# A sorted-row store for the last stage's gathers: 832 rows gathered once and loaded per tile, in place of 960 gathers

## The chip, the core and the metric

The kernel runs on one core of a Trainium2 chip. The metric is the device time of one execution in microseconds (us), from start to end. Engines are named as in the profile: PE is TensorE (PEld its weight loads), DVE is VectorE, ACT is ScalarE, POOL is GpSimd and SP is SyncE, which here issues DMAs and computes nothing. A "q" behind an engine's name marks its sequencer, which waits, branches, does arithmetic on registers and issues DMAs.

## What is computed

Four graph layers follow each other on 6250 nodes of 128 features and 106250 edges (`src`, `dst`, sorted by `dst`): a gated graph network, a hypergraph layer, an attention layer and an edge network. The change lies in the last one:

```python
def _L3_gnn_ref(x, edge_index, We1, be1, We2, be2, Wn1, bn1, Wn2, bn2):
    src, dst = (edge_index[0], edge_index[1])
    e_in = jnp.concatenate([x[src], x[dst]], axis=-1)
    edge_new = _mlp(e_in, We1, be1, We2, be2)
    agg = jax.ops.segment_sum(edge_new, dst, num_segments=x.shape[0])
    mesh_new = _mlp(jnp.concatenate([x, agg], axis=-1), Wn1, bn1, Wn2, bn2)
    return x + mesh_new
```

The first product of the edge network splits in a source part and a target part. The kernel makes both per node, so an edge needs one row of each: their sum, through a ReLU, is added up over the edges of a target.

## The kernel before

**Sorted rows and tiles.** Early in the kernel the edges are sorted by a key of their source's place (near, middle, far) and their target's block of 128 nodes, and stored in DRAM (`edges_halves`) as 832 rows of 128 edges. A tile is one row seen from one block of targets: a row that spans two blocks is in two tiles. There are T = 960 tiles, taken in 120 chunks of CH = 8. For each tile, `pair_idx` names its row and `pair_blk` its block; in the second hyperedge pass POOL fetches each tile's 128 edges (line 1770), VectorE splits them in target and source (`pair_steps`, lines 983 to 999), and TensorE turns them so that `local` (target inside the block) and `gather_idx` (source) stand with edges on partitions (`pairs_kept`).

**Source rows.** The attention pass (pass 5) writes the source part of 13 groups of nodes to a DRAM `table` (SP, line 546). POOL gathers by `gather_idx` (line 1148), one indirect DMA for the 128 edges of a tile, 64 KB. `early_pool` runs beside the attention pass: 20 pairs of chunks, 16 gathers each, into `x_fm`, where each pair waits for the groups that its sources need (`early_need`, line 1162) and is stored to `early_rows` in DRAM by POOL (line 1158). `edge_pool` then gathers the other 80 chunks straight into a ring of HOT = 4 slots, each slot when line 1306 has used it.

**The stage between.** After the attention pass ScalarE copies turned node rows to `x_fm` (line 1984, 25 chunks); copy 10 waits until all early stores have landed, as it overwrites their place. Then all engines meet, and the edge stage starts.

**The edge stage.** Six chunks make a turn in the order "DDEDDE" (D: direct, E: from `early_rows`); 20 turns. Per chunk, SP loads the targets inside the block, broadcast to all partitions (line 1198, 512 KB of f32), and in E chunks the stored rows (line 1191). ScalarE makes from the targets a one-hot matrix (`turned_hots`, lines 1219 and 1221); TensorE multiplies it with the block's target part (line 1272); VectorE adds the gathered source rows (line 1306, twice per chunk, counted in `edge_pre`); ScalarE applies the ReLU (line 1236); TensorE sums by target (lines 1248 and 1252) and VectorE adds to `acc` (line 1314). TensorE and VectorE read block numbers from a table in SBUF to registers (`registers`, line 477). SP's waits for one chunk come in program order, ahead of its DMAs. Behind the stage follow the node network, the last normalization and the output.

Of the kernel before, what the change touches and what calls it, by code (L numbers as in the profile page):

```python
# [20 lines left out]
P = 128  # L21
# [18 lines left out]
HOT = 4  # L40
# [28 lines left out]
EARLY = 40  # L69
EARLY_PAIRS = EARLY // 2  # L70
DIRECT = CHUNKS - EARLY
TURN = "DDEDDE"
LOOPS = EARLY // TURN.count("E")
PER_TURN = TURN.count("D")
SPARE = DIRECT - PER_TURN * LOOPS
assert EARLY % 2 == 0 and LOOPS * TURN.count("E") == EARLY and SPARE >= 0 and HOT == PER_TURN
# [80 lines left out]
def gnn(nc, d):  # L157
    ctx = ExitStack()
    with ctx:
# [49 lines left out]
        block_row = block_of[0:1, :]  # L209
# [82 lines left out]
        early_need = sb("early_need", [1, EARLY_PAIRS], I32)  # L292
        early_f = sb("early_f", [1, EARLY_PAIRS])

# [45 lines left out]
        pair_rows, pair_key = pair_rows.bitcast(I32), pair_src.bitcast(I32)  # L340
# [4 lines left out]
        early_ring = [x_fm[:, TW + KT * P + k * CH * P:TW + KT * P + (k + 1) * CH * P] for k in range(4)]  # L345
        early_twos = [x_fm[:, TW + KT * P + 2 * k * CH * P:TW + KT * P + 2 * (k + 1) * CH * P] for k in range(2)]
# [10 lines left out]
        early_rows = dram("early_rows", (EARLY, P, CH * P))  # L357
# [4 lines left out]
        local_rows = dram("local_rows", (TP, P))  # L362
# [22 lines left out]
        def S(name):  # L385
            if name not in made:
# [5 lines left out]
        half_landed = [S(f"half_landed{k}") for k in range(2 * HOT)]  # L392
        early_in = [half_landed[2 * (HOT - 2 + k)] for k in range(2)]
        direct_landed = [Count(half_landed[k], (16 * 2 * CH * ((EARLY_PAIRS + 1 - (k // 2 - HOT + 2)) // 2)
                                                if k in (2 * HOT - 4, 2 * HOT - 2) else 0)) for k in range(2 * HOT)]
# [5 lines left out]
        early_stored = Count(S("pairs_in"), 16 * TG)  # L401
# [41 lines left out]
        def col(j):  # L443
# [5 lines left out]
        targets = [stage[:, (4 + k) * CH * P:(5 + k) * CH * P] for k in range(2)]  # L449
        assert 6 * CH * P <= NBP * W and HOT * CH * P <= NP and HOT * CH <= 2 * SC  # L450
        row_ring = [big[:, NP + k * CH * P:NP + (k + 1) * CH * P].rearrange("p (t f) -> p t f", f=P) for k in range(HOT)]
        EARLY_SLOTS = TURN.count("E")
        early_ready = [big[:, NP + (HOT + k) * CH * P:NP + (HOT + k + 1) * CH * P].rearrange("p (t f) -> p t f", f=P)
                       for k in range(EARLY_SLOTS)]
# [9 lines left out]
        assert (HOT + EARLY_SLOTS) * CH * P + T // WINDOW <= NP and GW <= EC and GROUPS < LOOPS and 2 * len(TURN) % 3 == 0  # L464
        assert len(TURN) % HOTS == 0 and len(TURN) % 2 == 0
# [38 lines left out]
        early_landed = [Count(tile_landed[k], 16 * -(-(turns_before(len(MODES)) - k) // RING)) for k in range(EARLY_SLOTS)]  # L504
# [35 lines left out]
        def matrix_sp(p, sp):  # L540
# [31 lines left out]
            if p == SCALED:  # L572
                scale_load((GROUPS - 1) % 2, GROUPS - 2)
                sp.wait_ge(S("pair_values"), 1)
                sp.dma_start(local_rows.rearrange("(g p) e -> p g e", p=P), pair_f).then_inc(S("local_stored"), 16)
                sp.wait_ge(S("local_stored"), 16)
# [261 lines left out]
        def matrix_pe(p, pe):  # L838
            mode = MODES[p]

            def body(n, g, first_turn, i):
                wait(pe, S("group_out"), groups_before(p) + n - 1 + LOOPED * i)
                for t in range(TURNS):
# [4 lines left out]
                    if p == SCALED and n == 0 and t == 10:  # L848
                        pe.wait_ge(S("pair_values"), 1)
                        for v, values in enumerate((pair_f, pair_src)):  # L850
                            for b in range(TG):
                                last = nc.tensor.transpose(ps[:, 1 + 2 * v + b // 4, (b % 4) * P:(b % 4 + 1) * P],
                                                           values[:, b, :], ident[:, :])
                        last.then_inc(S("pair_flipped"), 1)
# [64 lines left out]
        def matrix_dve(p, dve):  # L919
# [61 lines left out]
            def pair_keys():  # L981
                one = chain(dve)
                dve.wait_ge(S("pairs_in"), 16 * TG)
                one(nc.vector.tensor_scalar(pair_key, pair_rows, (1 << KEY_BITS) - 1, None, ALU.bitwise_and))
                one(nc.vector.tensor_scalar(pair_rows, pair_rows, KEY_BITS, None, ALU.logical_shift_right))

            def pair_locals():
                for b in range(TG):
                    last = nc.vector.tensor_scalar(pair_f[:, b, :], pair_key[:, b, :], pair_blk[:, b:b + 1], None, ALU.subtract)
                chain(dve)(last)  # L990

            def pair_from():
                chain(dve)(nc.vector.tensor_scalar(pair_src, pair_f, 0.0, None, ALU.is_ge))

            def pair_below():
                chain(dve)(nc.vector.scalar_tensor_tensor(pair_src, pair_f, float(P), pair_src, ALU.is_lt, ALU.mult))

            def pair_sources():
                nc.vector.tensor_tensor(pair_src, pair_rows, pair_src, ALU.mult).then_inc(S("pair_values"), 1)
            pair_steps = [pair_keys, pair_locals, pair_from, pair_below, pair_sources]  # L1000

            def pairs_kept():
                dve.wait_ge(S("pair_flipped"), 1)
                for v, out in enumerate((local, gather_idx)):
                    for j in range(2):
                        last = nc.vector.tensor_copy(out[:, j * 4 * P:(j + 1) * 4 * P], ps[:, 1 + 2 * v + j, :])
                last.then_inc(S("pair_flipped"), 1)
# [67 lines left out]
        class Spot:  # L1075


            def __init__(self, i, h, x=0, nodes_done=False):
                self.i, self.h, self.x = i, h, x
                self.nodes = not x and not nodes_done and h == len(TURN) - 1  # L1080
                self.nodes_done = nodes_done or x
                self.u = len(TURN) * i + h + x
                self.known = isinstance(i, int)
                self.direct = x > 0 or TURN[h] == "D"
                if x:
                    self.k = PER_TURN * LOOPS + x - 1
                    self.u = len(TURN) * LOOPS + x - 1
                    self.use = self.k // HOT
                else:
                    before = TURN[0:h].count(TURN[h])  # L1090
                    self.k = TURN.count(TURN[h]) * i + before
                    self.use = i
                self.slot = (TURN[0:h].count("D") if self.direct else TURN[0:h].count("E")) if not x else self.k % HOT
                self.par = (x - 1) % 2 if x else h % 2
                self.hot = (x - 1) % HOTS if x else h % HOTS
                self.at = x - 1 if x else h
                self.pair = (len(TURN) * LOOPS + x - 1) // 2 if x else len(TURN) // 2 * i + h // 2
                self.chunk = EARLY + self.k if self.direct else self.k
                self.first = self.known and not x and i == 0 and h == 0
                self.last = x == SPARE if SPARE else self.known and i == LOOPS - 1 and h == len(TURN) - 1  # L1100

            def after(self):
                if self.x:
                    return Spot(0, 0, self.x + 1)
                if self.h + 1 < len(TURN):
                    return Spot(self.i, self.h + 1)
                return Spot(0, 0, 1) if self.known and self.i == LOOPS - 1 else Spot(self.i + 1, 0)

            def before(self):
                if self.x > 1:  # L1110
                    return Spot(0, 0, self.x - 1)
                if self.x == 1:
                    return Spot(LOOPS - 1, len(TURN) - 1)
                return Spot(self.i, self.h - 1) if self.h else Spot(self.i - 1, len(TURN) - 1)

            def q_bank(self, g):
                return ps[:, 4 + (2 * self.at + g) % 3, :]

            def rows(self):
                return row_ring[self.slot] if self.direct else early_ready[self.slot]  # L1120

            def wait_rows(self, eng, g):
                if self.direct:
                    wait(eng, direct_landed[2 * self.slot + g], 64 * (self.use + 1))
                elif g == 0:
                    wait(eng, early_landed[self.slot], 16 * (self.use + 1))

        def edge_turns(eng, body):

            def turn(i, nodes_done=False):  # L1130
                for h in range(len(TURN)):
                    body(Spot(i, h, 0, nodes_done))
# [7 lines left out]
        def direct_at(k):  # L1140

            if k >= PER_TURN * LOOPS:
                return len(TURN) * LOOPS + k - PER_TURN * LOOPS
            spots = [h for h in range(len(TURN)) if TURN[h] == "D"]
            return len(TURN) * (k // PER_TURN) + spots[k % PER_TURN]

        def gather(pool, out, t):
            return nc.gpsimd.indirect_dma_start(out, None, table[0:N, :], bass.IndirectOffsetOnAxis(gather_idx[:, t:t + 1], 0))  # L1148

# [1848 lines left out]
```

## Time and profile before

| what | value |
| --- | --- |
| time, median of 3 runs | 4566.51 us (4559.16 to 4568.67) |
| the profiled execution's own time | 4566.38 us |
| its span, first to last instruction | 4564.6 us |
| busy, PE / DVE / ACT / POOL | 84% / 72% / 51% / 58% |
| POOL in the last 850 us (from 3700) | 0.95 us busy of each 1.26 |
| chain that ended last, largest part | POOL line 1148, 13% into `big` and 5% into `x_fm` |

The page gives each engine's busy time as a share of the span; stages differ much in what limits them. The chain is followed back from the last instruction to what released each step. In a group's line the idle time stands behind the bar, with what ended most of it. All stretches below are in us from the span's start.

### The profile page before, as it was taken

The numbers are of one execution on the slowest core, as the hardware profiler recorded it, in microseconds if no ns is written. First come the engines' busy times: TensorE is split into PE (matmuls) and PEld (weight loads), VectorE is DVE, ScalarE is ACT, GpSimd is POOL, SyncE is SP. The second block draws the span as 40 slices with busy tenths as digits, with TensorE's granted clock in tenths as the row PEclk, the third lists the DMA queues.
The fourth block names the chain that finished last, engine by engine and source line by source line (L and its number), as shares of the span: only waits on it lengthen the run. The fifth ranks groups of instructions, "written<-read, shape, count | busy, mean of one in ns | idle before, by whom it ended". The sixth has DMA issues, their size and how long they took to land. (4 is left out here: it accounts for less than half of the span.)

```text
span 4564.6 us, 82617 instructions
## 1 busy us (share of the span) xinstructions
PE 3855.8 (84%) x24477; PEld 3205.3 (70%) x24478; DVE 3281.3 (72%) x7175; ACT 2334.1 (51%) x3120; POOL 2669.8 (58%) x2702
## 2 busy tenths in 40 slices
PE   5888408998889998998699799789999988888777
PEld 3666207776667776777488588479999976666665
DVE  6887898897788888887776543557887865555556
ACT  0000306665455555553555555578888855555545
POOL 3777777777377777777730000000477777777773
PEclk8999759999999999999799799789999989888888
DMA  9920009998538845982598788214677755454543
GB/s 381 373 95 1 3 0 329 366 368 298 200 116 282 269 144 179 291 280 88 173 299 297 171 296 297 99 56 143 194 235 242 242 164 163 151 160 158 158 154 97
DMA packets 362569, 914.64 MB, mean 200 GB/s; under 512 B 113834, under 2 KB 138524, under 8 KB 362291
## 3 DMA queue, kind: packets, MB, share of 16 engines
q1 hardware_dynamic: 213570, 645.89, 42.8%
q10 hardware_dynamic: 58609, 180.13, 10.3%
q0 software_dynamic: 90112, 85.23, 7.9%
q8 instruction: 136, 2.23, 0.2%
q14 instruction: 142, 1.16, 0.1%
HBM read 701.50 MB, written 209.51 MB: 200 GB/s over the span
## 5 line engine op out<-in xcount | busy, mean ns | idle before, releaser
L1765 POOL DMA_INDIRECT edges_halves<-local,gather_idx x832 | 850.9, 1023 | 304.7 <-issue 253.4
L1704 POOL DMA_INDIRECT adj_t<-cell_val,cell_at x832 | 815.6, 980 | 321.6 <-issue 321.6
L878 PE MATMUL ps<-tiles_r,stage_r 128*128 128x512 f32 x2028 | 808.4, 399 | 43.2 <-ACT tiles_r L813 34.5
L1148 POOL DMA_INDIRECT x_fm<-table,gather_idx x320 | 340.9, 1065 | 793.7 <-DMA table<-cell_at 689.1
L1148 POOL DMA_INDIRECT big<-table,gather_idx x640 | 611.2, 955 | 195.0 <-issue 194.1
L813 ACT CAST tiles_r<-onehot 128x1024 fp32r<-128x1024 f16 x338 | 355.0, 1050 | 292.7 <-DMA onehot<-adj_t 152.1
L718 DVE TENSOR_SCALAR_CACHE_REDUCE big<-ps 128x512 f16<-128x512 f16 (+2 forms) x724 | 429.5, 652 | 81.9 <-PE ps L670 65.7
L878 PEld LDWEIGHTS ps<-tiles_r,stage_r 128*128 128x128 f32 x2028 | 386.0, 190 | 145.2 <-issue 27.6
L885 PE MATMUL ps<-stage,big 128*128 128x130 f32 x4046 | 466.6, 277 | 17.9 <-DVE big L1039 16.1
L885 PEld LDWEIGHTS ps<-stage,big 128*128 128x128 f32 x4046 | 461.3, 193 | 18.6 <-issue 12.8
L1306 DVE TENSOR_TENSOR stage<-ps,big 128x512 f32<-128x512 f32 x240 | 161.4, 687 | 347.3 <-DMA big<-table,gather_idx 315.2
L771 ACT ACTIVATE big<-big,cols,stage 128x512 f32 (+1 forms) x508 | 371.6, 803 | 66.0 <-PE ps L885 53.0
L880 PE MATMUL ps<-tiles_r,lower_r 128*128 128x512 f32 x1016 | 400.7, 395 | 0.0
L880 PE MATMUL ps<-tiles_r,lower_late 128*128 128x512 f32 x1012 | 399.4, 395 | 0.0
L1272 PE MATMUL ps<-big,stage 128*128 x1920 | 285.7, 311 | 76.5 <-DVE stage L1306 29.7
L1272 PEld LDWEIGHTS ps<-big,stage 128*128 128x128 f32 x1920 | 264.0, 220 | 103.3 <-issue 102.9
L2083 PE MATMUL ps<-big,ident_h 128*128 128x104 bf16 (+1 forms) x2880 | 318.5, 247 | 9.2 <-issue 8.9
L1049 DVE CAST tiles_r<-onehot 128x1024 fp32r<-128x1024 f16 x338 | 245.4, 727 | 106.2 <-PE ps L880 90.0
L1236 ACT ACTIVATE stage<-stage 128x512 f32<-128x512 f32 x240 | 148.2, 627 | 336.6 <-DVE stage L1306 332.0
L878 PE MATMUL ps<-rows_r,stage_r 128*128 128x512 f32 x676 | 269.7, 399 | 38.1 <-ACT rows_r L813 36.1
L2083 PEld LDWEIGHTS ps<-big,ident_h 128*128 128x128 bf16 x2880 | 228.1, 101 | 101.3 <-issue 15.9
L2466 DVE TENSOR_TENSOR big<-ps,stage 128x1248 bf16<-128x1248 f32 x192 | 271.0, 1453 | 26.8 <-PE ps L2083 25.9
(490 smaller groups left out, 8199.6 us busy)
## 6 DMA issues: line engine op xcount, KB each, us to landing
onehot<-adj_t SPq DMA_DIRECT2D x332, 512.0 KB
big<-adj_t SPq DMA_DIRECT2D x332, 512.0 KB
onehot<-adj_s SPq DMA_DIRECT2D x170, 512.0 KB
adj_t<-rows ACTq DMA_DIRECT2D x13, 6656.0 KB
adj_s<-big ACTq DMA_DIRECT2D x157, 512.0 KB
stage<-local_rows SPq DMA_DIRECT2D x120, 512.0 KB
big<-adj_s SPq DMA_DIRECT2D x84, 512.0 KB
x_fm<-adj_s SPq DMA_DIRECT2D x84, 512.0 KB
```

The costliest lines, as they stand in the source:

```text
L718: last = nc.vector.tensor_scalar(turned[turn % RING][:, j, of, :].rearrange("p m c -> p (m c)"), flips[turn % 2][:, j, of, :].rearrange("p ...
L771: nc.scalar.activation(tile32[s][:, m * GW:(m + 1) * GW], r_rows[:, bass.ds(g * GW, GW)], ACT.Relu, bias=col(MINUS_ONE), scale=stage_nm[:, ...
L813: nc.scalar.copy(tile_r[s][:, 0:TW // 2], raw_tile(p, s)[:, 0:TW // 2]).then_inc(S("cast_act"), 1)
L878: nc.tensor.matmul(psum_fm(p, n)[:, 0:cut], upper_rows[:, k, :], tile[:, 0:cut], start=k == 0, stop=False, skip_group_check=True)
L880: last = nc.tensor.matmul(psum_fm(p, n)[:, 0:cut], lower_of(p)[:, k, :], tile[:, 0:cut], start=False, stop=k == NBP - 1, skip_group_check= ...
L885: last = nc.tensor.matmul(psum_nm(p, n, j), tile[:, j * P:(j + 1) * P], stage_nm[:, k, 0:AW], start=k == 0 and j % 2 == 0, stop=k == NBP - ...
L1148: return nc.gpsimd.indirect_dma_start(out, None, table[0:N, :], bass.IndirectOffsetOnAxis(gather_idx[:, t:t + 1], 0))
L1272: last = nc.tensor.matmul(spot.q_bank(g)[:, (u % 4) * P:(u % 4 + 1) * P], ring_ohT[:, h * CH + u, :], q_nm[:, bass.ds(blk[u] * P, P)], sta ...
L1704: nc.gpsimd.indirect_dma_start(out, bass.IndirectOffsetOnAxis(cells[:, c:c + 1], 0), cell_val[:, c:c + 1], None).then_inc(S(name), 16)
L1765: nc.gpsimd.indirect_dma_start(edges_halves, bass.IndirectOffsetOnAxis(slot_at[:, at:at + 1], 0), slot_val[:, at:at + 1], None).then_inc(h ...
L2083: return nc.tensor.matmul(ps[:, bank, of], stationary, moving, start=False, stop=True, skip_group_check=True)
L2466: nc.vector.tensor_tensor(eq[done % 4], own_keys(n).unsqueeze(1).to_broadcast([P, SHIFTS, SLW]), bass.AP(behind.tensor, behind.offset, [be ...
```

## The change

Each of the 832 sorted rows (EDGE_ROWS) is gathered once. `rows_pool` takes 52 pairs of 8 rows: 16 gathers into one of two rings (the first BESIDE = 20 pairs in `x_fm`, the others in `big` and `stage`), then a store of 1 MB to `edge_rows` in DRAM, one 64 KB block per row. Four gathers into the next pair it issues the store, and eight gathers later it waits for the store's landing and counts `rows_kept` up. There are no direct chunks and no turn of "DDEDDE" any more; all 120 chunks are alike.

Per chunk SP loads the targets, now in bf16 (256 KB), then loads 8 row numbers from a table in SBUF to registers, loads the number of the pair that must be stored and waits for it, waits for the slot (a ring of SLOTS = 3), and issues 8 DMAs of 64 KB, one per tile, from `edge_rows` at the row's number. ScalarE's copy 10 waits for `rows_kept` of 20.

The row numbers come with two more matmuls and some VectorE steps where the block numbers are made (before 691 us), go through `block_of` and are copied to tables in `edge_tables`, at the start of VectorE's part of the stage between; the block tables move there too, from the start of the edge stage. The sources are now read by two plain DMAs of whole rows instead of per tile, and limited to N - 1.

```diff
-HOT = 4
+SLOTS = 3
...
-EARLY = 40
-EARLY_PAIRS = EARLY // 2
-DIRECT = CHUNKS - EARLY
-TURN = "DDEDDE"
...
+SPOTS = 6
+LOOPS = CHUNKS // SPOTS
+EDGE_ROWS = P * EC // P
+ROW_GROUPS = EDGE_ROWS // CH
+ROW_PAIRS = ROW_GROUPS // 2
+BESIDE = 20
...
-        early_rows = dram("early_rows", (EARLY, P, CH * P))
+        edge_rows = dram("edge_rows", (EDGE_ROWS, P, P))
...
-        local_rows = dram("local_rows", (TP, P))
+        local_rows = dram("local_rows", (TP, P), BF16)
...
+        def rows_pool(pool):
...
             def store(k):
-                pool.wait_ge(early_in[k % 2], 16 * 2 * CH * (k // 2 + 1))
-                nc.gpsimd.dma_start(early_rows[2 * k:2 * k + 2].rearrange("k p e -> p k e"),
-                                    early_twos[k % 2].rearrange("p (k e) -> p k e", k=2)).then_inc(early_stored.sem, 16)
...
+                wait(pool, rows_in[k % 2], 16 * 2 * CH * (k // 2 + 1))
+                nc.gpsimd.dma_start(edge_rows[2 * CH * k:2 * CH * (k + 1)].rearrange("r p f -> p r f"),
+                                    pair_ring[k % 2 + 2 * (k >= BESIDE)].rearrange("p (r f) -> p r f", f=P)).then_inc(rows_out.sem, 16)
+
+            def stored(k):
+                wait(pool, rows_out, 16 * (k + 1))
+                pool.sem_inc(rows_kept.sem, 1)
+
+            for k in range(ROW_PAIRS):
                 pool.wait_ge(table_stored.sem, pool.value_load(early_need[0:1, k:k + 1], min_val=table_stored.base + 16 * NEAR_RANKS,
                                                                max_val=table_stored.base + 16 * GROUPS))
...
+                if k == BESIDE:
+                    wait(pool, table_stored, 16 * GROUPS)
+                    pool.wait_ge(S("weight_act"), KT * PASS_TURNS)
+                to = pair_ring[k % 2 + 2 * (k >= BESIDE)]
                 for u in range(2 * CH):
                     if u == CH // 2 and k > 0:
                         store(k - 1)
...
+                    if u == CH + CH // 2 and k > 0:
+                        stored(k - 1)
+                    r = 2 * CH * k + u
+                    nc.gpsimd.indirect_dma_start(to[:, u * P:(u + 1) * P], None, table[0:N, :],
+                                                 bass.IndirectOffsetOnAxis(gather_idx[:, r:r + 1], 0)).then_inc(rows_in[k % 2].sem, 16)
...
         def edge_sp(sp):
...
-            wait(sp, early_stored, 16 * EARLY_PAIRS)
-            for slot in range(EARLY_SLOTS):
-                early(slot, slot, None)
+            row_regs.extend(sp.alloc_register(f"row{u}") for u in range(CH))
+            wait(sp, tables_ready, 1)
 
             def body(spot):
                 wait(sp, S("hot_turned"), spot.u - 1)
                 sp.dma_start(targets[spot.par], local_rows[bass.ds(CH * spot.chunk, CH), :].rearrange("(a t) e -> a (t e)", a=1)
                              .to_broadcast([P, CH * P])).then_inc(targets_landed[spot.par], 16)
...
+                sp.load(row_regs, row_table[0:1, bass.ds(CH * spot.chunk, CH)])
+                rows = [sp.snap(r, min_val=0, max_val=EDGE_ROWS - 1) for r in row_regs]
+                sp.wait_ge(rows_kept.sem, sp.value_load(need_table[0:1, bass.ds(spot.chunk, 1)], min_val=rows_kept.base + 1,
+                                                        max_val=rows_kept.base + ROW_PAIRS))
+                sp.sem_inc(rows_opened, 1)
+                wait(sp, S("edge_pre"), 2 * (spot.u - SLOTS) + 2)
+                for u in range(CH):
+                    sp.dma_start(row_ring[spot.slot][:, u, :], edge_rows[bass.ds(rows[u], 1), :, :].rearrange("a p f -> p (a f)")
+                                 ).then_inc(half_landed[2 * spot.slot + u // WINDOW], 16)
...
             for c in range(REAL_CHUNKS):
                 wait(act, F("flip_done", "_x3"), c + 1)
-                if c == (TW + KT * P) // CN:
-                    wait(act, early_stored, 16 * EARLY_PAIRS)
+                if c == beside_at // CN:
+                    wait(act, rows_kept, BESIDE)
...
+            edge_tables(dve)
             for c in range(REAL_CHUNKS):
                 edge_taken(c, c % 2)
```

## Rows read from the trace of the kernel before

**Rows 1.** The page: chain by line, then costliest groups (busy, mean ns | idle, releaser).
```profile
POOL big L1148 13%; PE ps L885 7%; POOL x_fm L1148 5%; PE ps L2275 1%; PE ps L2282 0%; POOL early_rows L1158 0%; DMA big<-table,gather_idx 0%; PE ps L2262 0%; PE ps L2264 0%; DVE st L2938 0%; DVE big L2960 0%; POOLq L1162 0%; DVE big L1039 0%; DMA onehot<-adj_s 0%; PE ps L903 0%
...
L1306 DVE TENSOR_TENSOR stage<-ps,big 128x512 f32<-128x512 f32 x240 | 161.4, 687 | 347.3 <-DMA big<-table,gather_idx 315.2
```
**Rows 2.** Line 1148 (count; ns min/median/max, first and last start in us; forms).
```profile
L1148 POOL DMA_INDIRECT big<-table,gather_idx x640: 946/952/1177, 3700.9 to 4505.9; - x160
L1148 POOL DMA_INDIRECT x_fm<-table,gather_idx x320: 946/987/1473, 3238.0 to 3697.0; - x160
```
**Rows 3.** Timeline of POOL, two stretches (start, duration, what, idle before).
```profile
3659.53 0.76 POOL L1158 DMA_DIRECT2D early_rows<-x_fm  x1
3660.60 0.99 POOL L1148 DMA_INDIRECT x_fm<-table,gather_idx  x1 [0.30 <-issue]
...
4504.62 0.95 POOL L1148 DMA_INDIRECT big<-table,gather_idx  x1 [0.30 <-issue]
4505.88 0.95 POOL L1148 DMA_INDIRECT big<-table,gather_idx  x1 [0.30 <-issue]
```
**Rows 4.** Line 1158, POOL's store of a pair.
```profile
L1158 POOL DMA_DIRECT2D early_rows<-x_fm x20: 755/758/797, 3267.8 to 3699.8; - x20
```
**Rows 5.** Timeline of VectorE, three chunks near the start of the edge stage.
```profile
3743.47 1.33 DVE L1306 TENSOR_TENSOR stage<-ps,big 128x512 f32<-128x512 f32 x2
...
3747.67 1.29 DVE L1306 TENSOR_TENSOR stage<-ps,big 128x512 f32<-128x512 f32 x2
...
3751.82 1.46 DVE L1306 TENSOR_TENSOR stage<-ps,big 128x512 f32<-128x512 f32 x2
```
**Rows 6.** Timeline of SP in the edge stage, two DMAs behind each other.
```profile
4113.83 0.34 SPq L1198 DMA_DIRECT2D stage<-local_rows  x1
4114.47 0.33 SPq L1191 DMA_DIRECT2D big<-early_rows  x1
```
**Rows 7.** SP's instructions of lines 1198 and 146 (the value of a wait).
```profile
L1198 SPq DMA_DIRECT2D stage<-local_rows x120: 328/333/433, 3720.9 to 4493.4; - x120
L1198 SPq FUSED_REGOPS  x108: 52/55/85, 3744.2 to 4452.1; - x108
...
L146 SPq FUSED_REGOPS  x36: 42/43/43, 3757.9 to 4452.7; - x36
```
**Rows 8.** Line 599, a register load, its arithmetic and its assertion on SP.
```profile
L599 SPq TENSOR_LOAD <-need x13: 270/525/797, 691.0 to 1162.3; - x13
L599 SPq FUSED_REGOPS  x13: 147/147/189, 691.6 to 1162.6; - x13
L599 SPq SEQ_ASSERT  x13: 18/18/37, 691.8 to 1162.8; - x13
```
**Rows 9.** Line 477, register loads on TensorE's queue (8 from `rows`, 2 from `big`).
```profile
L477 PEldq TENSOR_LOAD <-rows x120: 587/591/614, 3724.1 to 4500.9; - x120
L477 PEldq TENSOR_LOAD <-big x120: 542/547/569, 3734.0 to 4512.7; - x120
```
**Rows 10.** Timelines of POOL, ScalarE and SP around the start of the edge stage.
```profile
3697.04 0.95 POOL L1148 DMA_INDIRECT x_fm<-table,gather_idx  x1 [0.30 <-issue]
...
3700.89 0.99 POOL L1148 DMA_INDIRECT big<-table,gather_idx  x1 [0.30 <-issue]
...
3707.85 0.37 ACT L1984 COPY x_fm<-ps 128x256 f32<-128x256 f32 x1 [0.36 <-PE ps L2303]
...
3720.07 0.82 SPq L1191 DMA_DIRECT2D big<-early_rows  x2
```
**Rows 11.** The chain in order of time: two landings of gathers (start, duration).
```profile
3943.23 2.51 DMA big<-table,gather_idx
...
4505.88 4.76 DMA big<-table,gather_idx
```
**Rows 12.** SP's waits from 690 to 1200 us (total, times, longest).
```profile
SPq L593 <- POOLq L1718: 31.7, 2, 22.3
```
**Rows 13.** The view of DMAs, one issue (count, KB each, us to landing).
```profile
local_rows<-big SPq DMA_DIRECT2D x1, 512.0 KB, 6.7
```

More of the change, by code:

```diff
@@ L391, in gnn @@
         targets_landed = [S(f"targets_landed{k}") for k in range(2)]
[L392 to L395, printed above, removed]
+        half_landed = [S(f"half_landed{k}") for k in range(2 * SLOTS)]
+        halves_written = [Count(S(f"at_written{k}"), 16 * sum(UNITS[k::2])) for k in range(2)]
+        rows_in = [Count(halves_written[k].sem, halves_written[k].base + 16 * SLW * (SL // 2)) for k in range(2)]
+        rows_out = Count(S("pairs_in"), 16 * (TG + 2))
+        rows_kept, tables_ready = [Count(S(name), NC * GRU_LAYERS) for name in ("n_ready", "r_ready")]
         turned_stored = [S(f"turned_stored{s}") for s in range(RING)]
@@ L448, in gnn @@
         ring_e = stage[:, 2 * CH * P:4 * CH * P].rearrange("p (t e) -> p t e", e=P)
[L449 to L454, printed above, removed]
+        targets_at = NP + (SLOTS + 2) * CH * P
+        targets = [big[:, targets_at + k * CH * P // 2:targets_at + (k + 1) * CH * P // 2].bitcast(BF16) for k in range(2)]
+        assert 6 * CH * P <= NBP * W and (SLOTS + 3) * CH * P + T // WINDOW <= NP
+        pair_ring = [x_fm[:, beside_at + k * 2 * CH * P:beside_at + (k + 1) * 2 * CH * P] for k in range(2)] +             [big[:, NP + SLOTS * CH * P:NP + (SLOTS + 2) * CH * P], stage[:, 4 * CH * P:6 * CH * P]]
+        row_ring = [big[:, NP + k * CH * P:NP + (k + 1) * CH * P].rearrange("p (t f) -> p t f", f=P) for k in range(SLOTS)]
+        row_table = rows_flat[32:33, CH * P:CH * P + T].bitcast(I32)
+        need_table = rows_flat[32:33, CH * P + T:CH * P + T + CHUNKS].bitcast(I32)
         HOTS = 3
@@ L849, in body @@
                         pe.wait_ge(S("pair_values"), 1)
[L850 to L853, printed above, removed]
+                        for b in range(TG):
+                            nc.tensor.transpose(ps[:, 1 + b // 4, (b % 4) * P:(b % 4 + 1) * P], pair_f[:, b, :], ident[:, :])
+                        for b in range(whole):
+                            nc.tensor.transpose(ps[:, 3 + b // 4, (b % 4) * P:(b % 4 + 1) * P], pair_src[:, b, :], ident[:, :])
+                        last = nc.tensor.transpose(ps[:, 3 + whole // 4, (whole % 4) * P:(whole % 4) * P + left],
+                                                   pair_src[0:left, whole, :], ident[0:left, 0:left])
                         last.then_inc(S("pair_flipped"), 1)
@@ L1002, in pairs_kept, with row_limits @@
+            def row_limits():
+                for of, g in row_parts:
+                    last = nc.vector.tensor_scalar(pair_src[of, g, :], row_src[of, g, :], float(N - 1), None, ALU.min)
+                last.then_inc(S("pair_values"), 1)
+            pair_steps = [pair_keys, pair_locals, pair_halves, row_sources, row_limits]
             def pairs_kept():
                 dve.wait_ge(S("pair_flipped"), 1)
-                for v, out in enumerate((local, gather_idx)):
+                for v, (out, most) in enumerate(((local, TP), (gather_idx, EDGE_ROWS))):
@@ L1005, in pairs_kept @@
                     for j in range(2):
-                        last = nc.vector.tensor_copy(out[:, j * 4 * P:(j + 1) * 4 * P], ps[:, 1 + 2 * v + j, :])
+                        end = min((j + 1) * 4 * P, most)
+                        last = nc.vector.tensor_copy(out[:, j * 4 * P:end], ps[:, 1 + 2 * v + j, 0:end - j * 4 * P])
                 last.then_inc(S("pair_flipped"), 1)
@@ L1075, in gnn @@
         class Spot:
[L1078 to L1082, printed above, removed]
-                self.known = isinstance(i, int)
[L1084 to L1100, printed above, removed]
@@ L1102, in after, with __init__ @@
-            def after(self):
[L1103 to L1107, printed above, removed]
-            def before(self):
[L1110 to L1114, printed above, removed]
+            def __init__(self, i, h, nodes_done=False):
+                self.i, self.h = i, h
+                self.nodes = not nodes_done and h == SPOTS - 1
+                self.nodes_done = nodes_done
+                self.u = self.chunk = SPOTS * i + h
+                self.known = isinstance(i, int)
+                self.par, self.hot, self.slot = h % 2, h % HOTS, h % SLOTS
+                self.use = SPOTS // SLOTS * i + h // SLOTS
+                self.pair = SPOTS // 2 * i + h // 2
+                self.first = self.known and i == 0 and h == 0
+                self.last = self.known and i == LOOPS - 1 and h == SPOTS - 1
@@ L1122, in wait_rows @@
             def wait_rows(self, eng, g):
[L1123 to L1126, printed above, removed]
+                wait(eng, half_landed[2 * self.slot + g], 64 * (self.use + 1))
         def edge_turns(eng, body):
             def turn(i, nodes_done=False):
-                for h in range(len(TURN)):
-                    body(Spot(i, h, 0, nodes_done))
+                for h in range(SPOTS):
+                    body(Spot(i, h, nodes_done))
@@ L1138, in edge_turns @@
             turn(LOOPS - 1, True)
[L1140 to L1148, printed above, removed]
-        def early_pool(pool):
+        def rows_pool(pool):
             pool.wait_ge(S("pair_flipped"), 2)
@@ L1265, in body @@
                 blk = kept(pe, f"block{h}")
-                if not spot.x and spot.h == 0:
+                if spot.h == 0:
                     wait(pe, node_kept, GROUPS if spot.nodes_done else spot.i)
@@ L1753, in _ @@
             pool.wait_ge(stage_end, ended["first"])
-            halves_written = [Count(S(f"at_written{k}"), 16 * sum(UNITS[k::2])) for k in range(2)]
             def sorted_there(n):
```

127 lines of the change are left out of this document (58 added, 69 removed).

## The prediction

> **What bounds the kernel now.** I read the chain of waits first, then the costliest groups, then the last 850 us engine by engine. POOL's gathers of line 1148 hold 13% and 5% of the span on the chain, more than any other line [rows 1]. They come in two runs: 320 "early" ones from 3238.0, beside the attention pass, and 640 "direct" ones from 3700.9 to 4505.9, through the edge stage [rows 2]. In the second run a gather follows the last every 1.26 us (0.95 busy, 0.30 issue) [rows 3], so 640 take 806 us. The consumer waits: line 1306 of VectorE, which adds gathered rows to the target part, sat idle 315.2 us before its 240 instructions for gathers to land [rows 1]. Where rows had come in ahead, at the stage's start, a chunk of 8 tiles took 4.0 to 4.2 us (3743.47 to 3747.67 to 3751.82) [rows 5], against 6.6 us over the whole stage (790 us from SP's first DMA at 3720.07 to the last landing, for 120 chunks) [rows 10, 11]. So the edge stage is bound by POOL, with some 300 us to be had if nothing else came late. The last gather lands at 4505.88 + 4.76 = 4510.64 [rows 11]; 54.0 us of span remain behind it. The profiled execution took 4566.4, 1.8 over its span and level with the median of 4566.5; my sums run on its time axis and add 1.8.
>
> **The change, part by part.**
>
> *Gathers.* 128 of 960 vanish. At 1.26 us in the edge stage that is 161 us of POOL time.
>
> *Stores on POOL.* 20 stores become 52. The old one costs 0.758 us [rows 4] and adds nothing more to the cadence: 3659.53 to 3660.60 is its 0.76 plus the usual 0.30 [rows 3]. The old store has 2 x 128 = 256 pieces of 4 KB; the new one has 16 x 128 = 2048 pieces of 512 B, as a row lies in 64 KB of its own. No row shows such a store. From below, its price s is 0.76 if pieces don't count; from above 0.758 x 8 = 6.06 if only they do. A gather has 128 pieces and takes 0.95, so fewer pieces are not cheaper, which leans to the low end: I take s = 2.0, and keep 0.76 and 6.06.
> The trace's 0.758 stands beside a rule of the Trainium skill ("DMA: Bandwidth & Descriptors", section "Anatomy of one DMA — SWDGE (gpsimd) path"): many descriptors can be emitted before generating them costs noticeably more. By it s would be near 0.76 and the forecast below some 22 us less; no row here has two sizes of a store to test it.
>
> *Row loads on SP.* This is the part that I think decides. SP issued per chunk one DMA for the targets and, one chunk in three, one of stored rows. Now it issues nine, each with an address from a register, and loads registers twice, all in order on one sequencer. From rows:
>  - one such DMA: two that follow each other start 0.64 us apart (4113.83, 4114.47) [rows 6], and between them lies one wait's value, 0.043 [rows 7], with its gap; the DMA instruction alone is 0.333 and its address arithmetic 0.055 [rows 7]. I take 0.54. Nine are 4.86 us.
>  - eight row numbers by one register load: SP's loads took 0.270 to 0.797, median 0.525 [rows 8]; eight registers in one load cost TensorE's queue 0.591 where two cost 0.547 [rows 9], so I add 0.05. With address and bounds arithmetic (0.055 and 0.147) and gaps: 0.90.
>  - the pair that must be stored by then: another load, 0.525 + 0.147 + 0.018 [rows 8], address and gaps: 0.92.
>  - three waits with their values: 0.22.
> Sum: 6.90 us per chunk, 6.4 with both loads at their shortest, 7.45 at their longest. 120 chunks are 828 us; 13 small degree loads and 19 loop ends add about 12. So SP needs 840 us for what POOL's 806 us now bounds, and nothing of it can be started before the stage: SP passes the stage boundary first, as in the trace, where its first edge DMA goes out at 3720.07 [rows 10]. SP rarely waits inside: body u waits for the sum of chunk u-3 and the turned targets of u-2, and both are done some 8 us before, as a chunk needs 4.2 us of compute and a landing about 2.5 [rows 5, 11].
> Here a rule of the Trainium skill speaks against the sum ("DMA: Bandwidth & Descriptors", section "Issuing engines are not separate DMA queues"): the sequencer's time to initiate a DMA is usually small beside the DMA. The rows above give 0.54 beside a landing of 2.5 to 4.8, which is small for one; whether nine in a row stay hidden is the second rival.
>
> *When the stage starts.* ScalarE's copy 10 of x_fm (line 1984) waited for the 20 early stores. It started unhindered at 3707.85, 12.2 us ahead of SP's first edge DMA [rows 10]. Now it waits until POOL has confirmed store 19, which sits 12 gathers and one store into pair 20. Pair 19's last gather started at 3697.04, so pair 20 could start at 3698.3 [rows 10], moved by 19 x (s - 0.76): 3721.9 at s = 2. Twelve gathers (15.1), the store (2.0) and a gap (0.3) give 3739.3, and 12.2 on SP starts at 3751.5, 31 us later than now. At s = 0.76 pair 20 waits for the last table store and starts at 3700.9, SP at 3729; at s = 6.06 SP starts at 3833.
>
> *The rest.* Block tables move from the stage's start to VectorE's transposing stage, where ScalarE's wait covers them. Two more matmuls and some VectorE steps in the table stage before 691 us lengthen it by about 6 us; the pass after it waits 31.7 us for POOL's scatter [rows 12], which swallows that. If that cover were gone: 6 us. Targets in bf16 halve 63 MB of traffic; transfers are not late. The pair arithmetic in the second hyperedge pass changes by about a microsecond, beside matmuls.
>
> **The sum.** SP starts at 3751.5, issues for 840 us, the last row lands 2.5 later (the short landing [rows 11]), and 54.0 follow: 4648, and with 1.8 of overhead 4650. POOL is off the path: at s = 2 its 512 gathers from 3721.9 take 645 and 32 stores 64, so it ends at 4430.7. Chunks use 6.93 rows per 6.9 us and POOL stores 16 per 22.2, so 320 rows of lead are never used up.
>
> **Rivals.**
> 1. *POOL's store near its upper bound.* s = 6.06: SP starts at 3833 and the same sum gives 4731. POOL's own path (below) comes to about the same, so both are late together. For it: 8 times the pieces, made by software. Against it: the gather's 0.95 for 128 pieces.
> 2. *The other side: SP's nine DMAs hide, and POOL still bounds, with 128 fewer gathers: faster.* Its point is SP's time per chunk: below 6.2 us the result is faster than 4566, and from 5.8 down POOL's path is the longer one. At s = 2 that is 4430.7, landing 3.8, store and its landing about 9 (a store of 0.5 MB landed in 6.7 us [rows 13]), three chunks that need the last 16 rows at up to 6.9 each, landing 2.5, tail 54.0: 4521, with the overhead 4522; at s = 0.76 about 4460. For it: at the loads' shortest SP is already at 6.4. Against: each of the nine DMAs is priced by instructions of the same kind in the same stage (120 for targets, of which 108 take their address from a register [rows 7]), and the sequencer does one thing at a time. The rule on initiating DMAs, named above, is this rival's case.
> 3. *The change does not relieve what waits.* Only if rows were not stored in time, so that SP stood at its wait for the pair. By the rates above that needs s over about 5 and is then rival 1.
>
> **How the numbers follow.** SP binds, 0.75: 4650, from 4567 (loads at 0.27, s = 0.76) to 4715 (loads at 0.80, s = 2). Most of it is slower (0.68); its low end gives 0.07 to no change. Store near its upper bound, 0.08: 4731, slower. SP hides, 0.17: 4458 to 4557, faster. That makes faster 0.17, same 0.07, slower 0.76, where 0.2% is about what a measurement of this kernel can tell from no change. The range runs from 4555, which leaves out nearly all of rival 2 (0.16), to 4731, with less than 0.04 above.
>
> **What would show it.** In the changed kernel SP's DMAs should stand in runs of nine with about 0.54 us from one to the next and a register load ahead of them; line 1306 should wait for DMAs of edge_rows that SP has just issued, with SP waiting for nobody; chunks 6.9 us apart; POOL's last gather near 4430, well before the end. If SP waits for POOL or for line 1306 most of the time, rival 2 holds. The store's duration on POOL settles s, and SP's first edge DMA (3751 here) the start. I am wrong above all if SP's DMA from a register costs less in a run of eight than its 0.54 between other work, or if the loads take 0.27.

## The result, and the profile after

| | before | after |
|---|---|---|
| median of four runs, us | 4563.7 | 4660.97 (4659.02 to 4662.1) |
| ratio to before | 1 | 1.0212 [1.0195, 1.0230] |
| span of the profiled execution | 4564.6 | 4657.0 (of 4659.02) |
| SP's first edge DMA | 3720.07 | 3768.65 |
| POOL's last gather starts | 4505.88 | 4427.20 |
| SP's last row DMA starts | none | 4605.53 |

The changed kernel is 97 us slower, though POOL ends 79 us sooner: the stage starts 48.6 us later and its last row load goes out 837 us after its first DMA, where 790 lay between that DMA and the last landing before.

The page of after: the chain by engine and by line, then the groups of the consumer (line 1286) and of two steps ahead of it (busy, mean ns | idle, releaser), which answer [rows 1].

```profile
SPq 12%; PE 9%; issue 5%; POOL 5%; DMA 2%; DVE 1%; ACT 1%; POOLq 0%; DVEq 0%; ACTq 0%
SPq L1190 8%; PE ps L888 7%; POOL x_fm L1155 5%; SPq L1183 1%; DMA big<-local_rows 1%; SPq L1185 1%; SPq L1177 1%; DMA edge_rows<-x_fm 1%; PE ps L2259 1%; PE ps L1254 0%; ACT stage L1201 0%; ACT stage L1203 0%; SPq L1184 0%; POOL edge_rows L1134 0%; DMA big<-edge_rows 0%
...
L1254 PE MATMUL ps<-big,stage 128*128 x1920 | 295.3, 318 | 211.8 <-ACT stage L1203 194.8
...
L1286 DVE TENSOR_TENSOR stage<-ps,big 128x512 f32<-128x512 f32 x240 | 164.7, 690 | 308.5 <-PE ps L1254 178.0 <-DMA big<-edge_rows 127.5 <-issue 2.5
L1201 ACT ACTIVATE stage<-big,cols 128x1024 f32<-128x1024 bf16 x120 | 137.8, 1148 | 422.7 <-DMA big<-local_rows 422.7
```

POOL's 13% for the gathers of the edge stage are gone. SP's queue, which was not in the list, holds 12%, 8% of it in line 1190, the row loads. Line 1286 (1306 before) still idles 308.5 us.

SP's queue in the timeline of after, from 4100 (start, duration; a run of equal instructions is one line): a chunk in which no instruction is unusually long.

```profile
4100.34 3.94 SPq L1190 DMA_DIRECT2D big<-edge_rows  x8
4104.49 0.33 SPq L1177 DMA_DIRECT2D big<-local_rows  x1
4106.71 0.33 SPq L1190 DMA_DIRECT2D big<-edge_rows  x1
```

Eight row DMAs take 3.94 us, so one follows the other every (3.94 - 0.33) / 7 = 0.515; the DMA of the targets stands behind them, and 2.22 later, after both register loads, the next chunk's first row goes out: 6.37 us for the chunk. What SP waited for from 3740 to 4640 (total, times, longest):

```profile
SPq L1177 <- DVEq L377: 68.2, 1, 68.2
SPq L143 <- ACT x_nm L1985: 18.0, 1, 18.0
SPq L1596 <- ACT x_nm L1985: 12.0, 5, 2.5
SPq L1177 <- ACT stage L1203: 0.2, 1, 0.2
```

The first is the wait for the stage's start, the next two lie in the last stage of the kernel: inside the edge stage SP waited 0.2 us in all. Its instructions by line (count, ns min/median/max, first and last start), which answer [rows 7, 8]:

```profile
L1190 SPq DMA_DIRECT2D big<-edge_rows x960: 332/333/1308, 3770.9 to 4605.5; - x192
...
L1183 SPq TENSOR_LOAD <-rows x120: 520/527/752, 3769.0 to 4600.4; - x120
...
L1185 SPq TENSOR_LOAD <-rows x120: 266/272/294, 3770.0 to 4601.1; - x120
```

The DMA instruction costs what the one before cost, 0.333; the load of eight row numbers 0.527, that of the needed pair 0.272. POOL's store by line, against [rows 4]:

```profile
L1134 POOL DMA_DIRECT2D edge_rows<-x_fm x20: 1205/1207/1217, 3263.1 to 3749.1; - x20
```

A store costs 1.21 us. The start of the stage in the timelines of POOL, ScalarE and SP, against [rows 10]:

```profile
3378.30 0.95 POOL L1155 DMA_INDIRECT x_fm<-table,gather_idx  x1 [51.23 <-DMA table<-big]
...
3743.10 0.95 POOL L1155 DMA_INDIRECT x_fm<-table,gather_idx  x1 [0.30 <-issue]
3744.36 0.95 POOL L1155 DMA_INDIRECT big<-table,gather_idx  x1 [0.30 <-issue]
...
3755.43 0.65 ACT L1967 COPY x_fm<-ps 128x256 f32<-128x256 f32 x2 [48.82 <-POOLq L1139]
...
3768.65 0.34 SPq L1177 DMA_DIRECT2D big<-local_rows  x1
```

POOL stood 51.2 us before its fifth pair (after 64 gathers), pair 20 began at 3744.36, and ScalarE's copy was let go at 3755.43. In the timeline of before POOL had stood there too, for 5.75 us and after 96 gathers:

```profile
3375.83 0.95 POOL L1148 DMA_INDIRECT x_fm<-table,gather_idx  x1 [0.30 <-issue]
3382.53 1.03 POOL L1148 DMA_INDIRECT x_fm<-table,gather_idx  x1 [5.75 <-issue]
```

The end of POOL and of SP in their timelines, against [rows 11]:

```profile
4427.20 0.95 POOL L1155 DMA_INDIRECT stage<-table,gather_idx  x1 [0.30 <-issue]
4431.40 1.21 POOL L1134 DMA_DIRECT2D edge_rows<-stage  x1 [3.25 <-DMA stage<-table,gather_idx]
...
4433.39 5.53 SPq L1190 DMA_DIRECT2D big<-edge_rows  x8
...
4601.92 3.95 SPq L1190 DMA_DIRECT2D big<-edge_rows  x8
```

POOL is done at 4432.6, 224 us before the end.

### The profile page after: what moved, and what is told of

Read it like the earlier page. It is cut to its first block and busy times, and to the rows that moved or that the text cites. A ratio compares the mean times of both kernels' runs of the same rounds, so it can differ in the third digit from the quotient of the medians.

```text
span 4657.0 us, 86389 instructions
## 1 busy us (share of the span) xinstructions
PE 3839.8 (82%) x24420; PEld 3208.0 (69%) x24481; DVE 3301.0 (71%) x7185; ACT 2327.2 (50%) x3120; POOL 2588.7 (56%) x2609
## 5 line engine op out<-in xcount | busy, mean ns | idle before, releaser
L1254 PE MATMUL ps<-big,stage 128*128 x1920 | 295.3, 318 | 211.8 <-ACT stage L1203 194.8
L1286 DVE TENSOR_TENSOR stage<-ps,big 128x512 f32<-128x512 f32 x240 | 164.7, 690 | 308.5 <-PE ps L1254 178.0
L1201 ACT ACTIVATE stage<-big,cols 128x1024 f32<-128x1024 bf16 x120 | 137.8, 1148 | 422.7 <-DMA big<-local_rows 422.7
L619 ACT CAST tiles_r<-onehot 128x2048 fp32r<-128x2048 f16 (+2 forms) x91 | 162.6, 1790 | 252.9 <-DMA onehot<-adj_t 223.7
```

The lines of the kernel that those rows point to most:

```text
L1254: last = nc.tensor.matmul(spot.q_bank(g)[:, (u % 4) * P:(u % 4 + 1) * P], ring_ohT[:, h * CH + u, :], q_nm[:, bass.ds(blk[u] * P, P)], sta ...
```

## The experiments

Theory A, the prediction's: SP's sequencer issues some 7 us of instructions per chunk in order, and 120 of these from the stage's start set the end. Theory B: the transfers set it (bytes or pieces, wherever they queue). Theory C: POOL does, by gathers and stores. Each of the ten kernels differs from the changed kernel by one edit, or in the last two by several; the lines that matter are shown, "..." stands for what is left out. The table gives medians, ratios to the kernel before as it ran beside each, and from the profiled executions (up to 9 us off the median) the starts of SP's first and last row DMA, the time between these, and the start of POOL's last gather.

| kernel | median | ratio, interval | first row DMA | last | between | POOL's last |
|---|---|---|---|---|---|---|
| after | 4661.0 | 1.0212 [1.0195, 1.0230] | 3770.9 | 4605.5 | 834.7 | 4427.2 |
| half_bytes | 4662.7 | 1.0206 [1.0189, 1.0223] | 3781.4 | 4617.7 | 836.3 | 4437.0 |
| two_loads | 4506.6 | 0.9864 [0.9848, 0.9881] | 3780.2 | 4452.0 | 671.9 | 4434.6 |
| targets_on_act | 4606.5 | 1.0085 [1.0068, 1.0103] | 3772.9 | 4554.2 | 781.3 | 4427.7 |
| one_load | 4733.1 | 1.0364 [1.0346, 1.0381] | 3771.7 | 4677.4 | 905.7 | 4426.4 |
| shifted_table | 4815.8 | 1.0540 [1.0518, 1.0561] | 3786.1 | 4768.8 | 982.7 | 4439.8 |
| need_by_shift | 4618.6 | 1.0116 [1.0094, 1.0139] | 3772.2 | 4556.6 | 784.4 | 4427.7 |
| earlier_start | 4626.9 | 1.0131 [1.0110, 1.0152] | 3726.9 | 4571.6 | 844.6 | 4432.2 |
| long_pieces | 4646.4 | 1.0185 [1.0167, 1.0203] | 3763.5 | 4589.5 | 826.0 | 4399.7 |
| all_three | 4512.4 | 0.9878 [0.9859, 0.9898] | 3726.5 | 4459.6 | 733.1 | 4433.3 |
| all_four | 4498.2 | 0.9861 [0.9840, 0.9882] | 3727.0 | 4448.5 | 721.4 | 4408.9 |

**half_bytes: do the bytes matter?**

```diff
-sp.dma_start(row_ring[spot.slot][:, u, :], edge_rows[bass.ds(rows[u], 1), :, :]...
+sp.dma_start(row_ring[spot.slot][:, u, 0:P // 2], edge_rows[bass.ds(rows[u], 1), :, 0:P // 2]...
```

> Each row DMA of SP moves only the first 64 of 128 columns, half the bytes, with as many DMAs and pieces as before it; the other half of what is added is left from earlier, so the output is not the reference's. Theory A (SP's issue): 4661, within 10 us. Theory B (transfers bound): the 512 KB of a chunk become 256 KB and the time falls by over 100 us. Theory C (POOL): 4661.

4662.7: no change. Line 1190 of this kernel:

```profile
L1190 SPq DMA_DIRECT2D big<-edge_rows x960: 332/333/2104, 3781.4 to 4617.7; - x192
```

The DMA instruction takes the same 333 ns for 32 KB as for 64. The bytes of the row loads are not what binds.

**two_loads: does the count of DMAs matter?**

```diff
-for u in range(CH):
-    sp.dma_start(row_ring[spot.slot][:, u, :], edge_rows[bass.ds(rows[u], 1), :, :]...
+for g in range(2):
+    sp.dma_start(row_ring[spot.slot][:, WINDOW * g:WINDOW * (g + 1), :],
+                 edge_rows[bass.ds(rows[WINDOW * g], WINDOW), :, :]...
```

WINDOW is 4. The needed pair goes by the fifth row number plus 3, and the row numbers end at EDGE_ROWS - 4.

> Per chunk SP issues two DMAs of four consecutive stored rows each (from the first and from the fifth row number) in place of eight of one row: the same bytes in the same 512 B pieces, six DMAs fewer on SP's sequencer. Where a row number repeats or skips within a half, the rows that are added are not the reference's. Theory A (SP's in-order issue bounds the stage): six times the 0.52 us from one row DMA to the next fall away, 3.1 of the 6.98 us per chunk; 3.85 us times 120 from 3768.7 would end SP near 4231, so POOL's stores take over: last gather at 4427, landing 3.8, store and its landing 9, three chunks at the compute's 4.2, landing 2.5, tail 51: about 4507, say 4490 to 4530. Theory B (the transfers, 512 B pieces or HBM, bound): within 0.2% of 4661. Theory C (POOL's gathers and stores bound): 4661 as well.

4506.6, where A said 4507. The same bytes in the same 512 B pieces, but issued by six instructions fewer, give back 154 us. This rules out B, and C for the changed kernel, as POOL's work is the same. The chain of this kernel by engine:

```profile
POOL 16%; PE 9%; issue 6%; DMA 2%; DVE 1%; POOLq 0%; ACT 0%; SPq 0%; DVEq 0%; ACTq 0%
```

What SP waited for from 3740 on:

```profile
SPq L1182 <- PE ps L1244: 117.1, 12, 11.2
...
SPq L1178 <- ACT stage L1205: 63.2, 48, 6.5
SPq L1188 <- POOLq L1139: 32.4, 3, 14.6
```

SP now waits for others, for POOL's stored pairs among them, and POOL is on the chain: the second rival's path, which lay hidden behind SP.

**targets_on_act: one DMA per chunk from another queue.**

```diff
 def edge_sp(sp):
...
-    wait(sp, S("hot_turned"), spot.u - 1)
-    sp.dma_start(targets[spot.par], ...)
...
 def edge_act(act):
...
+    def load_targets(spot):
+        act.dma_start(targets[spot.par], ...)
...
     def turned_hots(spot):
...
+        of = spot.after().after()
...
+            load_targets(of)
```

> The DMA of each chunk's targets is issued by ScalarE, behind its own use of the buffer, in place of SP; all else as it is. Theory A: SP loses 0.54 us per chunk (arithmetic, move and DMA with their gaps) and a wait: 120 times that is 65, so 4596, from 4580 to 4610. Theory B (transfers): the same bytes move, 4661. Theory C (POOL): 4661.

4606.5, 54.5 less; between SP's first and last row DMA 53.4 less, 0.445 a chunk where 0.54 was expected. The rest is in the register loads, which grew from 98.4 to 118.3 us in all, while the row DMAs fell from 372.4 to 364.0; when loads grow is told in the last section.

**one_load: nine registers at once.**

```diff
-sp.load(row_regs, row_table[0:1, bass.ds(CH * spot.chunk, CH)])
...
-sp.wait_ge(rows_kept.sem, sp.value_load(need_table[0:1, bass.ds(spot.chunk, 1)], ...
+sp.load(row_regs[0:CH + 1], row_table[0:1, bass.ds(spot.chunk, 1), :]...
...
+sp.reg_alu(row_regs[CH + 1], row_regs[CH], 1, ALU.max)
...
```

The table now holds nine values per chunk, eight rows and the pair.

> The eight row numbers and the needed pair stand side by side in one table and come with one register load of nine, in place of two loads. Theory A: SP loses the second load, its address and its assertion, 0.68 us in the chunk read, and gains one register operation of about 0.05: 120 times 0.62 is 75, so 4586, from 4570 to 4605. Theory B: 4661. Theory C: 4661.

4733.1: 72 us slower in place of 75 faster. All three theories missed. The one load became long:

```profile
L1183 SPq TENSOR_LOAD <-rows x120: 741/1871/4862, 3770.1 to 4671.4; - x120
```

Every fourth load took 0.75 (28 of 30), the others 1.87 and more. Nine values are 36 bytes, so every fourth chunk's begin at a multiple of 16 bytes from the table's start.

**shifted_table: the address alone.**

```diff
-row_table = rows_flat[32:33, CH * P:CH * P + T].bitcast(I32)
-need_table = rows_flat[32:33, CH * P + T:CH * P + T + CHUNKS].bitcast(I32)
+row_table = rows_flat[32:33, CH * P + 1:CH * P + 1 + T].bitcast(I32)
+need_table = rows_flat[32:33, CH * P + 1 + T:CH * P + 1 + T + CHUNKS].bitcast(I32)
```

> The table of row numbers begins 4 bytes later, so that each load of eight registers starts off a 16-byte boundary; nothing else differs. In the run with nine registers a load took 0.75 us where its address was a multiple of 16 bytes (every fourth chunk) and 1.87 at the others. If the address is the cause and theory A holds (SP's issue bounds): a load goes from 0.55 to some 1.6 to 1.85, 120 times 1.05 to 1.3 is 126 to 156, so about 4800, from 4780 to 4820. If the count of nine registers was the cause, or by theories B and C: 4661.

4815.8, as the address theory said (4780 to 4820). The same eight registers, 4 bytes further on:

```profile
L1183 SPq TENSOR_LOAD <-rows x120: 1663/1672/4909, 3783.0 to 4762.5; - x120
```

The load's median went from 0.527 to 1.672; 1.145 x 120 = 137 of the 148 us by which SP's stretch grew. One dearer instruction on SP per chunk goes into the time whole, which is theory A from the other side; as no DMA changed, it also speaks against a price per DMA that the transfers would pay.

**need_by_shift: no second load.**

```diff
-sp.wait_ge(rows_kept.sem, sp.value_load(need_table[0:1, bass.ds(spot.chunk, 1)], ...
+sp.reg_alu(need[0], row_regs[CH - 1], 0, ALU.max)
+sp.reg_alu(need[1], need[0], 4, ALU.logical_shift_right)
+sp.reg_alu(need[2], need[1], rows_kept.base + 1, ALU.add)
...
```

> The second register load of each chunk is dropped with its table; the pair that must be stored is worked out from the eighth row number by three register operations, and the eight-register load at 32-byte steps stays as it is. Theory A (SP's in-order issue bounds): 0.68 us of the second load with its address and assertion fall away, three operations of some 0.08 with their gaps come: 0.43 times 120 is 52, so 4609, from 4595 to 4625. Theory B (transfers) and C (POOL): 4661.

4618.6, in the range and 42 less; in the profiled execution, at 4610.2 the shortest of the four, SP's stretch is 50.3 shorter, 0.42 a chunk against 0.43 expected.

**earlier_start: the same chain, begun sooner.**

```diff
-BESIDE = 20
+BESIDE = 18
...
 if k == BESIDE:
+    store(k - 1)
     wait(pool, table_stored, 16 * GROUPS)
...
-    if u == CH + CH // 2 and k > 0:
+    if u == (6 if k == BESIDE else CH + CH // 2) and k > 0:
         stored(k - 1)
```

> 18 in place of 20 pairs go through the copy's buffers ahead of the edge stage, and the last of them is stored at once instead of four gathers into the next pair. Theory A (SP's chain of 120 chunks runs from its start to the end): the stage starts about 40 us sooner (SP's first edge DMA near 3729 in place of 3768.7) and the end comes by as much sooner: 4621, from 4608 to 4635. If something that keeps its own time bounds (POOL's gathers, which end at the same time or some 5 us later): 4661 or up to 5 more.

4626.9, 34 us less, with POOL's last gather 5 us later. The start moved by 44 (SP's first DMA at 3724.73); 10 of it were lost inside, where SP's stretch took 844.6. The row DMAs took 7 us less in all (365.0 for 372.4), but the register loads 13 more:

```profile
L1184 SPq TENSOR_LOAD <-rows x120: 521/527/2367, 3725.1 to 4566.4; - x120
...
L1186 SPq TENSOR_LOAD <-rows x120: 266/272/1367, 3726.1 to 4567.2; - x120
```

The medians are those of the changed kernel; 13 loads took 0.86 to 2.37, where the longest had been 0.75. All 13 start within 5 us of a store of POOL's.

**long_pieces: what a store's price goes by.**

```diff
-nc.gpsimd.dma_start(edge_rows[2 * CH * k:2 * CH * (k + 1)].rearrange("r p f -> p r f"), ...
+nc.gpsimd.dma_start(edge_rows[2 * CH * P * k:2 * CH * P * (k + 1), :].rearrange("(p r) f -> p (r f)", p=P), ...
```

With it SP's row DMAs read 128 pieces of 512 B at 8 KB steps, where a row had lain in one block of 64 KB.

> The stored rows of a pair lie partition by partition in device memory, so that a store writes 128 pieces of 8 KB in place of 2048 of 512 B, as many bytes; SP's row loads read 128 pieces of 512 B at 8 KB steps. If a store's price on POOL goes by its pieces (0.758 us at 256, 1.205 at 2048: 0.25 ns each): 0.73 us; POOL's last gather then starts 25 us sooner (4402), store 19 and with it SP's start 9 us sooner (3760 for the first row DMA at 3769.5). Theory A (SP's issue from its start): 4652, from 4645 to 4658. Theory C (POOL bounds): 25 us less, 4636. If the price goes by bytes or is SP's to pay for the strided reads: 1.2 us still, and 4661 or more.

4646.4, 14.6 less.

```profile
L1134 POOL DMA_DIRECT2D edge_rows<-big x16: 578/580/588, 3763.5 to 4384.9; - x16
```

The store fell to 0.58 with as many bytes, so its price goes with the pieces (the line through 256 and 2048 had given 0.73). POOL ends 27.5 sooner and the time falls by half of that, which speaks for A again: 7.4 come from the start. SP's stretch is 8.7 shorter, which A had at none: the row DMAs took 19 us less in all (353.1), the register loads 11 more (109.0).

**all_three and all_four: together.** The edits of targets_on_act, need_by_shift and earlier_start, then with long_pieces.

> Targets issued by ScalarE, no second register load, and the earlier start, together. Theory A: 6.08 us per chunk (6.96 less 0.45 and 0.43) times 120 is 730; from 3729 SP ends near 4459, and with a landing and a tail of 52 to 58 it is 4515; POOL's last rows (gathers until 4432, landing and store 13, three chunks at 5, landing and tail 55) give the same 4515. So 4515, from 4495 to 4535, below the kernel before (4566). Theories B and C: above 4615.

> The long pieces together with the targets on ScalarE, no second register load and the earlier start. With the three alone POOL's last store and SP's last chunk came due together (4512): the store's gain moves POOL's end 24 us ahead, SP's only by its start, some 8 us, since 18 stores ahead of it are shorter. Theory A: SP binds alone, 4504, from 4495 to 4512. If POOL alone had bound all three: 4490 or less.

4512.4 and 4498.2, both within their ranges, and faster than the kernel before by 1.2% and 1.4%. The chain of all_three at the end, in order of time:

```profile
4433.30 4.45 DMA stage<-table,gather_idx
4438.04 6.51 DMA edge_rows<-stage
4448.81 0.53 SPq L1180
...
4456.14 1.18 SPq L1189
...
4459.57 1.78 DMA big<-edge_rows
```

The last gather's landing, its store's landing and SP's last loads follow each other: POOL and SP are due together. With the long pieces SP's queue is on the chain again (12%) and POOL is not.

## Why the prediction was right

4650 was predicted, 4661.0 measured, for the reason given: SP's in-order issue took the place of POOL's gathers. That the sum came so near is luck in part: it had the start 17 us too early, the issuing from SP's first DMA to its last 3 and the tail behind it 5 too long, and the latter two give back half of the former; another 2 lie between the profiled execution and the median. In the ten kernels with one DMA per row, the changed one and all but two_loads, the span ended 50.3 to 52.7 us after the start of SP's last row DMA, while POOL's last gather lay 26 to 329 us ahead of that DMA.

- *Gathers.* 832 at the same 1.26 us; the last starts at 4427.20, where the prediction had POOL done at 4430.7. That agreement is luck in part: the cheaper store gave back what the later start took.
- *Stores, 0.76 to 6.06, taken at 2.0.* 1.21, so the first rival fell. The rule of the Trainium skill ("DMA: Bandwidth & Descriptors", "Anatomy of one DMA — SWDGE (gpsimd) path") pointed to the low end; the traces have 0.58 at 128 pieces, 0.758 at 256 [rows 4] and 1.21 at 2048. Sixteen times the pieces cost 2.1 times as much, much nearer to that rule than to a price per piece.
- *SP per chunk, 6.90.* The mean was right: from the first chunk's first row DMA (3770.85) to the last's (4601.92) are 119 chunks of 6.98, where the prediction had 840 / 120 = 7.00. Its make-up was not. A chunk without a long instruction took 6.37, just below the sum's low end of 6.4: nine DMAs at 0.515 in place of 0.54, and 1.73 for loads and waits where 2.04 were summed. That the mean agrees is luck: what filled it up was not in the sum: of the 742 row DMAs that SP issued before 4430, 82 took over 0.4 us, 50 us more than their 0.333 in all, and of the 208 after 4440 one did. Nearly all of the long ones start 1.8 to 4.8 us after a store of POOL's; behind the last store eight row DMAs took 5.53 (4433.39) in place of 3.95.
- *SP rarely waits.* Right: 0.2 us. The second rival fell with it: its point was 6.2 us per chunk. all_three, at 733.1 / 120 = 6.1 and with a start 44 us sooner, does come out faster than before.
- *The rule on initiating DMAs* (the Trainium skill, "DMA: Bandwidth & Descriptors", "Issuing engines are not separate DMA queues") fits each DMA by itself, 0.515 beside the 1.78 us that the last row of all_three took to land, and misleads for eight in order: two_loads saved 154 us by issuing alone.
- *Start, 3751.5 predicted, 3768.65 measured.* The step that failed is pair 20's start. With the real store price it gives 3698.3 + 19 x 0.45 = 3706.8; measured 3744.36. The 51.2 us before the fifth pair are the difference: POOL waits there for a part of the table that SP stores at 3375.1 (3377.1 before). In before it came to the same wait after 96 tiles, at 3376.8, and lost 5.8; now it came to it after 64 rows, at 3327.1. 51.2 less 5.8, less some 8 (shorter gathers, smaller gaps, a first gather 2.2 us earlier) are the 37.6. The prediction moved pair 20 by the stores alone and left out that 16 rows hold the work of more than 16 tiles, so that fewer gathers lie ahead of the same part of the table. That is read from these counts; no run tried it. Behind it the prediction was 6.3 too slow: the confirmation came not after twelve gathers but after eight, with the landing of store 19, 6.2 us after the store began, since POOL's sequencer had come to its wait before its engine had made the other gathers; ScalarE to SP took 13.2 for 12.2.
- *Tail.* 51.5 from SP's last row DMA to the end, for 2.5 + 54.0.
- *The rest.* The 6 us of the table stage were swallowed, as predicted: the first early gather starts at 3235.8, 2.2 us sooner than before [rows 2].
- *What would show it.* Line 1286 was said to wait for row DMAs. It did for 127.5 us; for 178.0 it waited for TensorE's line 1254, that for ScalarE's line 1203, and this follows line 1201, which idled 422.7 us for the targets' DMA. The prediction overlooked that the targets of the next chunk stand behind eight row loads in the same queue: late for the same reason, seen at another consumer.

## What to carry to other kernels

Price what a change moves onto a queue by instructions times their period, and set that sum beside the one it relieves: nine register-addressed DMAs and two register loads per chunk (6.98 us) outlast the 5.3 gathers per chunk (640 for 120 chunks, 6.7 us) that POOL made in the stage before, though each of them looks cheap and is off the path where it stands alone. A wait list in which the issuing queue waits for nobody, and a count experiment (the same bytes from fewer DMAs) beside a byte experiment, tell issue from transfer. When one queue binds, spread its instructions over another that has room, and look at once for the path that was second: here it stood at 4507, so that SP alone had 154 us to give.

## What the runs showed of the hardware that was not expected

- A load of eight registers on SP takes 0.527 us where it starts at a multiple of 16 bytes and 1.672 where it starts 4 bytes off; nine take 0.75 and 1.87, one takes 0.272. That fits 0.25 to 0.27 us for each 16 bytes when aligned (two, three and one of them), and 0.209 for each register when not (1.672 / 8, 1.871 / 9). Addresses are counted from the table's start. For a load of one register the address makes no difference: three of four begin off 16 bytes, and all 120 took 0.266 to 0.294.
- SP's instructions that start 1 to 5 us after a store of POOL's take longer, register loads as well as DMAs. In the changed kernel 81 of the 89 DMA instructions above 0.43 us (rows and targets) start within 4.8 us after a store, and take up to 1.31 in place of 0.333; no register load fell into that time, and none took over 0.75. In earlier_start and need_by_shift loads fell into it and took up to 2.37. What all row DMAs and loads took beyond 0.333 and beyond their medians, up to 4430, was 51 and 3 us in the changed kernel, 49 and 6 with half the bytes in the row loads, 33 and 14 with stores of 128 pieces in place of 2048. So neither the bytes of the row loads nor the pieces of the store change the sum much, and that the stores cause it is read from the times alone; what the two share is not shown. Stores are not all of it: with the targets issued by ScalarE, 27 of 78 row DMAs above 0.4 us lie over 5 us behind a store.
